# Moving the last block's values, the last transposes and some norms in a two-layer attention kernel

## The reference

```python
h = patches(x) @ W.T                                    # 64 x 49 x 192
h = layernorm(h + attention1(h))                        # 12 heads of 16, causal, bias on keys
def ffn(x):                                             # a second attention, with routed low-rank weights
    probs = softmax(x @ Wg.T + bg)                      # 8 experts
    top_w, top_idx = top_k(probs, 2)
    combine = scatter(top_w, top_idx)
    hw = (einsum('td,erd->ter', x, A) + ba) * combine
    delta = 2 * (einsum('ter,eor->to', hw, Bm) + combine @ bb)
    q, k, v = split(x @ Wqkv.T + bqkv + delta)
    return softmax(q @ k.T * 0.25) @ v @ Wproj.T + bproj
h = layernorm(h + ffn(h))
```

## Time and profile before

| What | Value |
|---|---|
| Median of three runs | 392.89 us |
| The profiled execution's own time | 392.47 us |
| Its span | 390.7 us |
| VectorE busy | 301.5 us (77%) |
| ScalarE busy | 218.5 us (56%) |
| GpSimd busy | 124.6 us (32%) |
| DMA, mean | 53 GB/s |

### The profile page before, as it was taken

The page is one execution under the profiler, slowest core; times in us unless marked ns, Lnnn a source line. Parts: engine busy times, 40 slices in busy tenths (PEclk is TensorE's granted clock), DMA queues, the critical chain, the costliest instruction groups (busy, mean ns, idle before and its releaser), DMA issues.

```text
span 390.7 us, 13738 instructions
## 1 busy us (share of the span) xinstructions
PE 373.3 (96%) x5312; PEld 327.3 (84%) x5312; DVE 301.5 (77%) x814; ACT 218.5 (56%) x692; POOL 124.6 (32%) x262
## 2 busy tenths in 40 slices
PE   5999999999999999999999999999999999989984
PEld 4888788988888898988889889888888978878973
DVE  7367777687777788987878888787798888698872
ACT  1344646564646645566655566655664565664642
POOL 1312422321433424133315233341325241423313
PEclk9999999999999999999999999999999999999999
DMA  8732522121131122210123201111011101110111
GB/s 269 232 99 62 137 55 54 36 55 48 20 110 24 26 39 73 81 59 9 18 66 70 66 8 29 17 31 22 21 17 29 29 21 19 18 33 14 25 36 37
DMA packets 49338, 20.68 MB, mean 53 GB/s; under 512 B 41262, under 2 KB 45713, under 8 KB 49274
## 3 DMA queue, kind: packets, MB, share of 16 engines
q1 hardware_dynamic: 45530, 10.43, 12.7%
q10 hardware_dynamic: 3744, 9.38, 7.6%
HBM read 12.57 MB, written 2.41 MB: 38 GB/s over the span
## 4 chain that ended last, share of the span: by engine, by line
PE 86%; DVE 5%; ACT 3%; issue 2%; DMA 2%; POOL 1%; SPq 0%; POOLq 0%; ACTq 0%
PE ps L494 12%; PE ps L572 9%; PE ps L599 9%; PE ps L610 7%; PE ps L584 6%; PE ps L621 5%; PE ps L544 4%; PE ps L548 4%; PE ps L546 4%; PE ps L622 4%; PE ps L524 3%; PE ps L530 2%; PE ps L528 2%; PE ps L566 2%; PE ps L642 2%; PE ps L632 2%
## 5 line engine op out<-in xcount | busy, mean ns | idle before, releaser
L965 DVE TENSOR_REDUCE psum<-probs 113x12 f32<-113x588 f32 x64 | 48.6, 760 | 33.9 <-ACT probs L808 33.9
L822 ACT COPY pt<-ps 113x339 f32<-113x339 f32 x128 | 50.2, 445 | 33.4 <-PE ps L599 32.8
L939 DVE TENSOR_REDUCE mx<-ps 113x12 f32<-113x588 f32 x64 | 48.7, 761 | 17.1 <-PE ps L572 16.6
L494 PE MATMUL ps<-tokw,xs 128*128 128x192 f32 (+1 forms) x300 | 56.3, 336 | 4.4 <-DMA tokw<-in_tokw 4.1
L443 POOL TENSOR_SCALAR shift<-mv,rstd 128x1 f32<-128x1 f32 (+1 forms) x50 | 14.2, 283 | 141.6 <-ACT rstd L857 141.6
L432 POOL TENSOR_SCALAR kbd<-k,const 64x294 f32<-64x294 f32 x64 | 34.7, 552 | 73.2 <-ACT q L801 67.5
L494 PEld LDWEIGHTS ps<-tokw,xs 128*128 128x128 f32 (+1 forms) x300 | 48.9, 192 | 7.1 <-DMA xs<-in_x 4.7
L599 PE MATMUL ps<-const,probs 113*113 113x113 f32 x384 | 50.0, 266 | 4.6 <-DVE probs L974 4.0
L599 PEld LDWEIGHTS ps<-const,probs 113*113 113x113 f32 x384 | 44.3, 178 | 9.5 <-issue 8.0
L974 DVE TENSOR_TENSOR probs<-probs,rsum 113x588 f32<-113x588 f32 x64 | 50.1, 782 | 2.2
L946 DVE TENSOR_TENSOR probs<-ps,mx 113x588 f32<-113x588 f32 x64 | 49.4, 772 | 2.2
(11 more groups left out here) (93 smaller groups left out, 785.0 us busy)
## 6 DMA issues: line engine op xcount, KB each, us to landing
xs<-in_x ACTq DMA_DIRECT2D x22, 384.0 KB, 3.8
vbd<-vrow SPq DMA_DIRECT2D x160, 18.4 KB
out<-o SPq DMA_DIRECT2D x24, 96.0 KB, 1.8
xs<-in_x SPq DMA_DIRECT2D x2, 384.0 KB, 6.4
tokw<-in_tokw ACTq DMA_DIRECT2D x3, 192.0 KB, 3.6
w<-in_w SPq DMA_DIRECT2D x1, 472.5 KB, 4.2
xs<-in_x SPq DMA_DIRECT2D x3, 128.0 KB, 3.4
add<-in_add SPq DMA_DIRECT2D x1, 361.5 KB, 7.2
```

The lines of the kernel that those rows point to most:

```text
L494: last = nc.tensor.matmul(ps[0:k, bank, 0:E], xs[:, b % XS, m, 0:k], tokw[:, m, :], start=(m == 0), stop=(m == KX - 1))
L822: nc.scalar.copy(pt[n % 2][:, 3 * half:3 * half + 3, :].rearrange("p g i -> p (g i)"), ps[0:PP, 2 + half, 0:3 * PP]).then_inc(pt_ready[hal ...
L939: nc.vector.tensor_reduce(mx[n % 2][:].rearrange("p (b h) -> p b h", b=2), score_view(n), AX.X, ALU.max).then_inc(mx_ready, 1)
L965: nc.vector.tensor_reduce(psum[:].rearrange("p (b h) -> p b h", b=2), probs_view(n), AX.X, ALU.add).then_inc(sum_ready, 1)
```

## The change

1. `h1_bank` gives bank 5 where a block projected in the slot is urgent. With h1 blocks in turn, that is slot 59 alone (block 24 of h1, with block 22's second projection).
2. Block 24's `project_v` moves from slot 61 to slot 62, behind the scores of slot 63, and writes to bank 7. The scores of slot 63 wait for 24 blocks of values instead of 25. `keep_busy`, which also writes bank 7, waits for all 25. ScalarE's copy of these values moves to slot 62, behind the second norm and ahead of the `yt` copy.
3. `inverse_deviation` of first norms stands ahead of the `yt` copy (and no longer behind it) where the next slot transposes this block and has no output projection: slots 5, 9, 17, 25, 33, 43 and 51.

```diff
 def h1_bank(n):
+    if any(urgent(b) for b in qkv2s(n)):
+        return 5
     return 6 if turns(n) and not qkv2s(n) else 4
...
-                        pe.wait_ge(L2.v_rows, BLOCKS)
+                        pe.wait_ge(L2.v_rows, BLOCKS - 1)
...
-            def project_v(L, b, parts, free):
+            def project_v(L, b, parts, free, bank=5):
...
             def keep_busy(count):
-                pe.wait_ge(hw_ready, BLOCKS)
+                pe.wait_ge(L2.v_rows, BLOCKS)
...
                     if n == LAST - 1:
                         scores(L2, attention(LAST)[1], LAST)
+                        project_v(L2, BLOCKS - 1, values2(BLOCKS - 1), (hw_ready, BLOCKS), 7)
...
+                    elif h1_bank(n) == 5:
+                        bank5 = transpose_h1(b, 5, bank5)
...
-                    bank5 = project_v(L2, b, values2(b), bank5)
+                    if b < BLOCKS - 1:
+                        bank5 = project_v(L2, b, values2(b), bank5)
...
-                    if urgent(b):
+                    if urgent(b) and b < BLOCKS - 1:
                         take_v(L2, b, 0, SLOT2)
...
+                if n == LAST - 1:
+                    take_v(L2, BLOCKS - 1, 0, SLOT2, 7)
+                norm_first = bool(turns1(n + 1) and not out1(n + 1) and not out2(n + 1))
+                if norm_first:
+                    for b in out1(n):
+                        inverse_deviation(L1, b)
                 if before:
                     take_y(n - 1, u)
...
-                for b in out1(n):
-                    inverse_deviation(L1, b)
+                if not norm_first:
+                    for b in out1(n):
+                        inverse_deviation(L1, b)
```

More of the change, by code:

```diff
@@ L583, in project_v @@
                 for m, (src, w) in enumerate(parts):
-                    last = nc.tensor.matmul(ps[0:k, 5, 0:E], src[:, 0:k], w[:, V0:V0 + E],
+                    last = nc.tensor.matmul(ps[0:k, bank, 0:E], src[:, 0:k], w[:, V0:V0 + E],
                                             start=(m == 0), stop=(m == len(parts) - 1))
@@ L808, in exponent, with take_v @@
                 nc.scalar.activation(p, p, ACT.Exp).then_inc(exp_ready, 1)
-            def take_v(L, b, at, slot_of):
+            def take_v(L, b, at, slot_of, bank=5):
                 k = tokens(b)
@@ L814, in take_v @@
                     act.wait_ge(pv_done, slot_of[last_tile(b - VR)] + 1)
-                nc.scalar.copy(L.vrow[b % VR][0:k], ps[0:k, 5, at:at + E]).then_inc(L.v_rows, 1)
+                nc.scalar.copy(L.vrow[b % VR][0:k], ps[0:k, bank, at:at + E]).then_inc(L.v_rows, 1)
             def take_pt(n):
```

## The result

The changed kernel took 390.91 us in the median of eight runs (389.84 to 391.3), the kernel before 392.36 in its eight: a ratio of 0.9947, with a 95% interval of 0.9927 to 0.9968. By this ratio it is 2.1 us less (1.3 to 2.9), while the two medians are 1.45 apart; 2.45 was forecast, and the time lies in the stated range. The profiled execution took 391.28 us over a span of 389.5, only 1.2 less than the span before.

What follows compares the result with a forecast made beforehand. TensorE, busy 96% of the span, was taken as the bound, so only its waits could be won: 1.30 (tail) + 1.0 + 0.15 (norms) = 2.45 us, from 392.89 to 390.4 us; range 389.4 to 391.8.

Steps and rivals of the forecast that it cites:

- What bounds it: Whole kernel: TensorE, busy 96% of the span, sets the pace; gains lie in its waits and carry to the end.
- Rival 4: Whole kernel: every wait removed comes back as another a few slots on; no effect, 392.9 us; chance 0.07.
- Bank 5: Slot 59: block 22's second projection no longer waits for the h1 copy; 0.64 us gained, bounds 0 and 0.64.
- every follower in rows 3 was idle: Slot 59's timeline: engines behind the projection, such as GpSimd, were idle, so they move with it; hence the full 0.64 us.
- The values: Slots 61 to 63: moving block 24's values removes the 1.13 us wait, leaving about 0.4 us for keys.
- The combined tail term: Slots 59 to 63: bank and values edits together bring slot 63's transposes 1.30 us earlier, bounds 0.64 and 1.76.
- Norms ahead of the yt copy: Seven slots: moved norms let the next h1 transposes start earlier; 1.0 us for slots 25 and 33, 0.15 for others.
- Moved, it follows the embedding's copy (170.57) as it followed the `yt` copy (171.07): 0.50 earlier: ScalarE, slot 25: the norm's pair starts directly behind the embedding's copy; 0.50 us gained per slot, slot 33 alike.
- rival 1: Slots 25 and 33: VectorE's hold on GpSimd and the late `yt` copy eat the norms' gain; 391.4 us; chance 0.18.
- rival 3: Slot 64: the last tile's values land too late and its weighing waits 3.7 us; 394.1 us; chance 0.04.

Runs made afterwards that it cites:

- e1_bank: Kernel before with only slot 59's h1 transposes in bank 5; ratio 0.9976 (0.9954 to 0.9999).
- e5_hold: Changed kernel with VectorE's scaling of slot 59 held until GpSimd has written slot 60's keys; slot 59 to 60 takes 7.04 us.
- e7_keys: Changed kernel with slot 63's keys ahead of block 19's norm on GpSimd; slot 61 to 63 takes 9.13 us, 9.38 in the changed kernel.
- e6_early: Changed kernel with the norm's pair of slots 25 and 33 ahead of the embedding's copy; 0.26 us gained in each.
- e8_late2: Changed kernel with one extra transfer ahead of each of tile 31's last two, two in all; the weighing waits 0.31 us.
- e10_changed: The changed kernel run again, unaltered, against the kernel before; 390.97 us, ratio 0.9958 (0.9942 to 0.9974).
- e4_late: Changed kernel with two extra transfers ahead of each of tile 31's last two, four in all; 397.18 us.

## Why the prediction was right, and where its sizes were off

**What bounds it: right.** Every gain came from a wait in the earlier trace rows, and each was carried from its slot to slot 64 without loss. Rival 4 falls.

**Bank 5: the wait right, size off (0.64 forecast, 0.41 measured).** The step that failed is "every follower in rows 3 was idle". GpSimd was idle, but its writes, moved 0.67 earlier against slot 59's transposes, came under VectorE's scaling, and the first took 0.27 longer. The scaling stood in the trace of before, from 357.41 to 358.18, just ahead of the writes at 358.45; I didn't lay the moved instruction over the other engines' times. e1_bank shows the wait with this edit alone, e5_hold takes it away by moving the scaling.

**The values: right (0.66 forecast, 0.61 measured; 0.60 alone).** The wait for the keys was put at 0.4 and measured at 0.36, VectorE's statistics decided slot 62's maximum, and both ways to slot 63's transposes arrived together. VectorE's added wait of 0.17 was missing from the forecast; it did no harm, as TensorE arrived then too. The limit by the keys is real: e7_keys gains 0.25 behind it. The combined tail term of 1.30 measured 1.02, all but 0.05 of the difference being bank 5's.

**Norms ahead of the yt copy: the wait right, two steps wrong (1.15 forecast; 0.66 in slots 25 and 33, and in the other five nothing that can be told).** In slots 25 and 33 the step that failed is "Moved, it follows the embedding's copy (170.57) as it followed the `yt` copy (171.07): 0.50 earlier". Between the two ScalarE issues a DMA for 0.33 us, which the timeline has as a row of its queue and which the busy rows leave out. So the pair moved 0.32, the column 0.31 to 0.33, and the gain was 0.33. Where an issue stands there it moved 0.32 to 0.34 (slots 5, 25 and 33), and 0.51 where none does (slots 17, 43 and 51). No run takes the issue away alone; this rests on the rows.

In slots 17, 43 and 51 the forecast was 0.05 each. The pair did move 0.51 there, but the column came under the scaling and lost all of it. This is rival 1's first half, in three slots where little was at stake. In slots 25 and 33, where rival 1 set it, it did not happen, and its other half, the late `yt` copy, did not come either.

Of the Trainium skill (SBUF — State Buffer, "Who interferes with whom"), the sentence that such an instruction is fully blocked until the other ends was weighed in the prediction at 0.3 per slot. That 0.33 was measured in slots 25 and 33 is chance: nothing was blocked there. Where a GpSimd instruction did start under the scaling, the traces nearly agree with the sentence. A column of 0.27 ended 0.13 behind the scaling's end. The larger ones of 0.50 ended 0.38 behind it, whether they had started 0.30, 0.40, 0.51 or 0.64 ahead of that end (e7_keys, changed kernel, e6_early, e5_hold). So all but some 0.13 of the work waited. The same section of the Trainium skill also says that whichever issues first keeps the port for its whole instruction. By the recorded starts it does not come out so: in slot 61 of the kernel before, a norm started 0.13 ahead of the scaling, at 369.72, and took 1.11 instead of 0.50, while the scaling took its usual 0.77.

**Too late values (rival 3): it did not happen.** The number behind it was loose, though: I took 1.8 us from issue to landing, and from the issue to the waiting matmul it was 2.1 and 3.5. The margin was 1.2 us by e8_late2.

**The sum.** 0.41 + 0.61 + 0.66 = 1.68, and the stretch of slots 1 to 64 shows 1.92, of which 0.12 is the step between slots 42 and 43, and 0.11 lies ahead of slot 26, where e1_bank has 0.10 with no edit. The first series gave 2.1 by its ratio (1.3 to 2.9), and e10_changed's gave 0.9958 (0.9942 to 0.9974), which is 1.65 us. By the stretches the forecast of 2.45 was 0.5 to 0.8 too much: 0.34 from the DMA issue, 0.15 from the columns of the other slots, 0.23 from bank 5's keys, and 0.05 from the values. The stated range, 389.4 to 391.8, took that in.

## What to carry to other kernels

When an instruction is moved earlier, read three rows at its new place: its own engine's, with the DMA issues in its queue, which count as busy nowhere; those of the engine that may hold it up (here VectorE's scaling for GpSimd); and its releaser's. A size that fits a theory doesn't show it. Two causes gave 0.33 here, and the time from the releaser's end to the start, 0.17 before and after, told which it was.

Measure edits of some tenths of a microsecond by stretches between fixed points of the trace: whole times of one kernel here spread by 1.5 us and more, while stretches of one slot without an edit agreed to 0.12, and mostly to 0.02.

A wait that is removed is worth what the next-latest input leaves of it: list, for the instruction that will run earlier, the time of each of its inputs. And a transfer's margin is measured by delaying it until somebody waits.

## What the runs showed of the hardware

- GpSimd's tensor_scalar and VectorE's tensor_tensor on two SBUF operands hold each other up, and in both directions. Under VectorE's subtraction, which reads one of its two operands from PSUM, a block norm took its usual 0.50 (changed kernel, from 173.49). A GpSimd instruction started under the scaling ended 0.13 us (128x1) or 0.38 (128x192, 64x294) behind its end, whether it had started 0.30 or 0.64 ahead of that end. A scaling that started among GpSimd's writes took 1.08 instead of 0.77 (e5_hold). A column started 0.10 ahead of the scaling ran in its usual 0.27 (e6_early), one started 0.03 ahead took 0.85.
- The issue of a 384 KB load on ScalarE took 0.33 us, and ScalarE's next instruction started 0.04 to 0.05 behind its end (changed kernel, slots 5, 25 and 33).
- The transposes of slot 1, which stand behind the first loads, started between 24.12 and 27.36 us in twelve profiled executions. What follows slot 64's took 9.7 to 9.8 in all but the two kernels with delayed values. In eleven of the twelve the whole difference stood already at the first transpose of h, at 8.78 to 9.95 us; e4_late was there at 10.90 and lost 1.1 more up to slot 1.
- Small transfers (49 rows, 18 KB or less) took 2.1 us from the start of their issue to the instruction that waited for them with two more in the queue, and 3.5 with four more.
